# A two-layer graph network with residual norm on one core: x is also read with features on partitions, TensorE turns no rows of it, and each layer has one PSUM pair

## The chip, the cores and the metric

The kernel runs on one core of one Trainium2 chip. The metric is the device time of one execution in microseconds (us). TensorE (PE) multiplies, with its weight loads (PEld) on the side; VectorE (DVE), ScalarE (ACT) and GpSimd (POOL) work elementwise, and SyncE (SP) mostly issues transfers between HBM and SBUF. Each engine has its own queue, which runs strictly in order; engines wait for one another by semaphores.

## What is computed

x has 100000 rows of 256 features; there are 25000 edges, sorted by dst. All is float32.

```python
def _sage_conv(x, src, dst, W_l, b_l, W_r):
    msgs = x[src]
    agg = jax.ops.segment_sum(msgs, dst, num_segments=N_NODES)
    deg = jax.ops.segment_sum(jnp.ones((src.shape[0],), x.dtype), dst, num_segments=N_NODES)
    mean = agg / jnp.maximum(deg, 1.0)[:, None]
    return mean @ W_l + b_l + x @ W_r
...
h = jax.nn.relu(_sage_conv(x, src, dst, W1_l, b1, W1_r))
h = jax.nn.relu(_sage_conv(h, src, dst, W2_l, b2, W2_r))
return h @ W3 + b3
...
x = _layernorm(x + _L0_gnn_ref(...), axis=-1)
```

## The kernel before

Every product is made in three matmuls of a rounded format: each operand is split into a high part (a cast on ACT) and a low part (the operand less its high part, on VectorE), and high × high, low × high and high × low are added in PSUM.

**Stages.** A short first stage splits the weights and works out, from the edge lists, the indices for the gathers, the ends of runs of equal dst, and the reciprocal degrees. The **main stage** handles all 100000 rows as if no edge ended in them: 196 groups g of 512 rows, four groups (slots u = 0 to 3) in each of 49 iterations i. Alongside, every iteration handles one batch of 512 edges: it gathers the rows x[src] and x[dst] (`xe`), turns them, sums the sources over runs of equal dst with a scan (`run`, `mean`), and stores layer-one results for both ends in `h_tab`. The **edge stage** then goes through the 49 batches again, makes layers two and three for the rows with edges, and scatters them over `out`.

**One group in the main stage.** SP loads 512 rows to `xn`. TensorE turns them (8 transposes of 128x128, helper `turn`, L851) into PSUM; ACT casts them to `xt_hi` (L480), VectorE subtracts to `xt_lo` (L645). Layer one is 12 matmuls of 512 columns (helper `columns`, L861). ACT adds the bias and applies relu in two halves to `h_full` in SBUF (L487), casts to `h_hi` (L489), VectorE subtracts to `h_lo` (L649). Layer two is the same again. Layer three is 24 matmuls of 256 columns by rows (helper `by_rows`, L872). VectorE adds `xb` = x + b3, which GpSimd made (L391), to `y` (L671), then takes moments (L683, L694); ACT takes the square root (L493) and normalises to `o` (L500), and SP stores it (L228).

**Order.** The order of each queue is written by hand in the functions named `body`. TensorE's is, for slot u: turn the rows of g+2, layer one of g+1, the edge work of this slot, layer three of g-1, layer two of g. The four PSUM pairs `pair0` to `pair3` rotate: x turned, layer one and layer two of one group lie in the same pair one after another, and edge work and layer three use the other two pairs. The edge work is: turn sources (u=0), turn destinations (u=1), a by-row layer for the sources (u=2, 24 matmuls), one for the destinations with their means (u=3, 48 matmuls). VectorE follows with `low_x` (g+2), `factors` (g-2), `low_h` of layer one (g+1), edge work, residual and moments of g-1, and `low_h` of layer two (g).

Of the kernel before, what the change touches and what calls it, by code (L numbers as in the profile page):

```python
# [5 lines left out]
P = 128  # L6
S = 4
G = S * P
# [5 lines left out]
def build(nc, x, src, dst, W1_l, b1, W1_r, W2_l, b2, W2_r, W3, b3, out):  # L14

# [12 lines left out]
    E = src.shape[0]  # L28
# [3 lines left out]
    NE = -(-E // G)  # L32
    EP = NE * G
    NT = EP // P
    Q = EP // 256
    QF, QR = E // 256, E % 256
    assert NG == NI * U and NE == NI and NT == 2 * Q and N < FAR and QF == Q - 1 and D == 256
    HALF = NE
    MIDDLE = HALF // 2
# [3 lines left out]
    with ExitStack() as ctx:  # L43
# [9 lines left out]

# [12 lines left out]
        xb = sb("xb", [P, 2, S, D])  # L66
        xt_hi = sb("xt_hi", [P, 2, K, G], f32r)
        xt_lo = sb("xt_lo", [P, 2, K, G], f32r)
        h_full = sb("h_full", [P, 2, K, G])
        h_hi = sb("h_hi", [P, 3, K, G], f32r)  # L70
        h_lo = sb("h_lo", [P, 3, K, G], f32r)
# [27 lines left out]
        idx = sb("idx", [P, 3, NT], i32)  # L99
# [4 lines left out]
        e_stage = sb("e_stage", [P, 2, S], i32)  # L104
        t_stage = sb("t_stage", [P, 3, S], i32)

        pair = [pb(f"pair{n}") for n in range(4)]

        pre = h_full[:, :, :, :].rearrange("p a k g -> p (a k g)")
        e_int = pre[0:Q, 0:1024].bitcast(i32).rearrange("p (a j) -> p a j", a=4)  # L110
        fill = pre[:, 1024:1824].bitcast(i32)
        e_f = y[:, :, :, :].rearrange("p a s d -> p (a s) d")[:, 0:4]
        p_src, p_dst, p_prev, p_next = (e_f[0:Q, n] for n in range(4))
        e_w = y[:, :, :, :].rearrange("p a s d -> p (a s) d")
        same, seg_last, count, whole = (e_w[0:Q, n] for n in range(4, 8))
        e_idx = o[:, :, :, :].rearrange("p a s d -> p (a s) d")[:, 0:3]
        tr = o[:, :, :, :].rearrange("p a s d -> p (a s d)")[:, 768:1152].rearrange("p (n c) -> p n c", n=3)
        ones = o[:, :, :, :].rearrange("p a s d -> p (a s d)")[:, 1152:1408]
        rdeg = o[:, :, :, :].rearrange("p a s d -> p (a s d)")[:, 1408:1664]
        rows3 = o[:, :, :, :].rearrange("p a s d -> p (a s d)")[:, 1664:2048].rearrange("p (n c) -> p n c", n=3)  # L120


        w_in, b_in, made, cleared, e_in = (sem(n) for n in ("w_in", "b_in", "made", "cleared", "e_in"))
# [3 lines left out]
        x_in = [sem(f"x_in{u}") for u in range(U)]  # L127
        y_out = [sem(f"y_out{b}") for b in range(2)]
        xt_ps, xhi_ok, xlo_ok = sem("xt_ps"), sem("xhi_ok"), sem("xlo_ok")
# [14 lines left out]
        stage_ok, tab_out, slot_in, slots_ok = (sem(n) for n in ("stage_ok", "tab_out", "slot_in", "slots_ok"))  # L144
# [14 lines left out]
        def after(eng, s, value):  # L159

            if not (isinstance(value, int) and value <= 0):
                eng.wait_ge(s, value)

        def rows(t, g):

            first = min(g * G, N - G) if isinstance(g, int) else g * G
            return t[bass.ds(first, G), :].rearrange("(p s) d -> p s d", s=S)

        def slots_of(t, j, start=0):
# [12 lines left out]

# [9 lines left out]

# [3 lines left out]

# [5 lines left out]
        def _(sp):  # L202
            sp.dma_start(xn[:, 0], rows(x, 0)).then_inc(x_in[0], 16)
            for n, w in enumerate((W1_r, W2_r, W3, W1_l, W2_l)):
                if n == 3:
                    sp.wait_ge(cleared, 5)
                sp.dma_start(w_raw[:, n], w.rearrange("(k p) n -> p k n", p=P)).then_inc(w_in, 16)
            sp.wait_ge(e_in, 16 * 9)
            for n, b in enumerate((b1, b2)):
                for k in range(K):  # L210
                    sp.dma_start(bias[:, n, k:k + 1], b[k * P:(k + 1) * P].rearrange("(p a) -> p a", a=1)).then_inc(b_in, 16)
            for row, b in ((b1_row, b1), (b3_row, b3)):
                sp.dma_start(row[:, :], b.rearrange("(a n) -> a n", a=1).to_broadcast([P, D])).then_inc(b_in, 16)
            for u in range(1, U):
                sp.dma_start(xn[:, u], rows(x, u)).then_inc(x_in[u], 16)

            sp.wait_ge(cleared, 6)
# [7 lines left out]

            def store(g, b):
# [3 lines left out]
            def edge_store(i, u):  # L230

                if u == 0:
                    sp.wait_ge(xdb_ok, i + 1)
                    sp.dma_start(slots_of(xdb_tab, i), xdb[:, :, :]).then_inc(xdb_out, 16)
                if u == 2:
                    sp.wait_ge(src_ok, i + 1)
                    sp.dma_start(slots_of(h_tab, i, EP), src_h[:, :, :]).then_inc(src_out, 16)
                if u == 3:
                    sp.wait_ge(dst_ok, i + 1)
                    sp.dma_start(slots_of(h_tab, i), dst_h[:, :, :]).then_inc(dst_out, 16)  # L240

            def body(i, first, last):
                for u in range(U):
                    g = i * U + u
                    if not last:
                        sp.wait_ge(xt_ps, (g + 1) * K)
                        sp.wait_ge(xb_ok, g + 1)
# [811 lines left out]
```

## Time and profile before

| | |
|---|---|
| median of 3 runs | 2999.09 us (2992.19 to 2999.65) |
| span of the profiled execution, first to last instruction | 2989.1 us |
| mean granted TensorE clock | 0.992 |
| busy, share of the span | PE 96%, PEld 86%, DVE 82%, ACT 67%, POOL 72% |
| main stage | about 35 to 2412 us |
| edge stage | about 2412 us to the end |

The span is measured inside one profiled execution, the median over separate runs of the whole; the difference of 10.0 us is what lies around the instructions. Busy shares are means over stages: what an engine's work is worth has to be read from the stage in which it stands.

### The profile page before, as it was taken

What the parts mean: (1) busy time and instruction counts of PE and PEld (TensorE: products, weight loads), DVE (VectorE), ACT (ScalarE), POOL (GpSimd) and SP (SyncE); (2) the same over time, 40 slices, a digit from 0 to 9 for tenths busy, and PEclk for the clock granted to TensorE, in tenths of its full rate; (3) what the DMA queues carried; (4) which work ended last, traced back from release to release, by engine and by line L of the source; (5) the groups of instructions that cost most, each with busy time, mean ns of one, the idle gap of its engine ahead of it and who ended that gap; (6) DMA issues with size and microseconds to landing.
All of it is one profiled execution on the core that took longest, in us unless ns stands there. A gap on an engine that the chain in (4) does not pass through costs nothing. (4 is left out here: it accounts for less than half of the span.)

```text
span 2989.1 us, 55620 instructions
## 1 busy us (share of the span) xinstructions
PE 2869.4 (96%) x18457; PEld 2581.4 (86%) x18457; DVE 2445.0 (82%) x4001; ACT 1997.4 (67%) x2992; POOL 2151.1 (72%) x1732
## 2 busy tenths in 40 slices
PE   5999999999999999999999999999999989999996
PEld 4888989898888889898988888898989879888885
DVE  5787887879787878878787878788787879899896
ACT  3676766767676767667676767676676746555554
POOL 5777777777776767667777767677777747777776
PEclk9999999999999999999999999999999999999998
DMA  4444444444444445444444444444444366666663
GB/s 131 151 152 145 162 150 149 154 142 161 152 155 148 153 143 165 149 148 154 143 159 154 155 147 153 145 164 149 148 154 145 130 205 232 235 223 226 238 221 141
DMA packets 253121, 488.25 MB, mean 163 GB/s; under 512 B 37615, under 2 KB 165206, under 8 KB 253090
## 3 DMA queue, kind: packets, MB, share of 16 engines
q1 hardware_dynamic: 202498, 387.58, 38.6%
q0 software_dynamic: 50176, 99.91, 10.3%
q10 hardware_dynamic: 416, 0.40, 0.0%
q8 instruction: 14, 0.23, 0.0%
q14 instruction: 17, 0.14, 0.0%
HBM read 284.67 MB, written 206.22 MB: 164 GB/s over the span
## 5 line engine op out<-in xcount | busy, mean ns | idle before, releaser
L487 ACT ACTIVATE h_full<-pair,bias 128x512 f32<-128x512 f32 x784 | 531.6, 685 | 681.2 <-PE pair L861 666.4
L649 DVE TENSOR_TENSOR h_lo<-h_full,h_hi 128x1024 fp32r<-128x1024 f32 x392 | 651.7, 1663 | 188.3 <-ACT h_hi L489 188.2
L391 POOL TENSOR_TENSOR xb<-xn,b_row 128x1024 f32<-128x1024 f32 x196 | 471.5, 2405 | 297.7 <-DVE y L671 295.9
L345 POOL DMA_INDIRECT xe<-in_x_dram,e_stage x392 | 500.9, 1278 | 176.9 <-issue 97.7
L872 PE MATMUL pair<-w_hi,h_hi 128*128 128x256 f32 x1960 | 565.4, 288 | 26.6 <-DVE h_lo L649 24.5
L872 PE MATMUL pair<-w_lo,h_hi 128*128 128x256 f32 x1960 | 555.3, 283 | 0.0
L872 PE MATMUL pair<-w_hi,h_lo 128*128 128x256 f32 x1960 | 555.2, 283 | 0.0
L489 ACT CAST h_hi<-h_full 128x1024 fp32r<-128x1024 f32 x392 | 412.0, 1051 | 12.5
L872 PEld LDWEIGHTS pair<-w_hi,h_hi 128*128 128x128 f32 x1960 | 375.6, 192 | 51.7 <-DVE h_lo L649 47.7
L500 ACT ACTIVATE o<-y,nb,rs 128x256 f32<-128x256 f32 x784 | 407.2, 592 | 5.6 <-DVE nb L702 5.3
L861 PE MATMUL pair<-xt_hi,w_hi 128*128 128x512 f32 x980 | 401.6, 410 | 7.9 <-DVE xt_lo L645 4.3
L861 PE MATMUL pair<-xt_lo,w_hi 128*128 128x512 f32 x980 | 385.4, 393 | 0.0
L861 PE MATMUL pair<-xt_hi,w_lo 128*128 128x512 f32 x980 | 383.9, 392 | 0.0
L872 PEld LDWEIGHTS pair<-w_lo,h_hi 128*128 128x128 f32 x1960 | 376.0, 192 | 1.9
L872 PEld LDWEIGHTS pair<-w_hi,h_lo 128*128 128x128 f32 x1960 | 376.0, 192 | 0.0
L671 DVE TENSOR_TENSOR y<-pair,xb 128x1024 f32<-128x1024 f32 x245 | 298.1, 1217 | 86.6 <-PE pair L872 82.2
L683 DVE BATCH_NORM_STATS2 stats<-y 128x6 f32<-128x256 f32 x980 | 344.0, 413 | 6.8
L851 PE MATMUL pair<-ident,xn 128*128 128x128 f32 x2352 | 306.2, 278 | 43.5 <-DMA xn<-h_tab,h_row 32.8
L851 PEld LDWEIGHTS pair<-ident,xn 128*128 128x128 f32 x2352 | 274.3, 142 | 76.1 <-issue 32.2
L861 PE MATMUL pair<-h_hi,w_hi 128*128 128x512 f32 x784 | 308.0, 393 | 0.0
L861 PE MATMUL pair<-h_hi,w_lo 128*128 128x512 f32 x784 | 307.8, 393 | 0.0
L861 PE MATMUL pair<-h_lo,w_hi 128*128 128x512 f32 x784 | 306.4, 391 | 0.0
(124 smaller groups left out, 6439.6 us busy)
## 6 DMA issues: line engine op xcount, KB each, us to landing
xn<-in_x_dram SPq DMA_DIRECT2D x196, 512.0 KB, 4.0
out_dram<-o SPq DMA_DIRECT2D x196, 512.0 KB, 2.6
seg<-seg_tab SPq DMA_DIRECT2D x74, 512.0 KB, 5.1
xdb_tab<-xdb SPq DMA_DIRECT2D x49, 512.0 KB, 4.8
h_tab<-src_h SPq DMA_DIRECT2D x49, 512.0 KB
h_tab<-dst_h SPq DMA_DIRECT2D x49, 512.0 KB, 6.3
xn<-h_tab SPq DMA_DIRECT2D x49, 512.0 KB, 5.1
xb<-xdb_tab SPq DMA_DIRECT2D x49, 512.0 KB, 4.1
```

The source lines that it names most:

```text
L345: nc.gpsimd.indirect_dma_start(out=xe[:, kind, s], out_offset=None, in_=x, in_offset=bass.IndirectOffsetOnAxis(ap=e_stage[:, kind, s:s + 1 ...
L391: nc.gpsimd.tensor_tensor(xb[:, b], xn[:, u], b3_row[:, :].unsqueeze(1).to_broadcast([P, S, D]), ALU.add).then_inc(xb_ok, 1)
L487: nc.scalar.activation(h_full[:, n, k], ps[:, k], ACT.Relu, bias=bias[:, n, k:k + 1]).then_inc(hf_ok[n], 1)
L489: nc.scalar.copy(h_hi[:, h], h_full[:, n]).then_inc(hhi_ok[n], 1)
L500: ins = nc.scalar.activation(o[:, b, s], y[:, b, s], ACT.Identity, bias=nb[:, b, s:s + 1], scale=rs[:, b, s:s + 1])
L649: nc.vector.tensor_tensor(h_lo[:, h], h_full[:, n], h_hi[:, h].bitcast(f32), ALU.subtract).then_inc(hlo_ok[n], 1)
L671: nc.vector.tensor_tensor(y[:, b].rearrange("p s d -> p (s d)"), ps[:, :, :].rearrange("p k g -> p (k g)"), xb[:, b].rearrange("p s d -> p ...
L683: ins = nc.vector.bn_stats(stats[:, s], y[:, b, s])
L851: ins = nc.tensor.transpose(ps[:, k, s * P:(s + 1) * P], rows_of[:, s, k * P:(k + 1) * P], ident[:, :])
L861: ins = nc.tensor.matmul(ps[:, m], wx[:, w, k, m * P:(m + 1) * P], a[:, k], start=first, stop=end)
L872: ins = nc.tensor.matmul(ps[:, s // 2, s % 2 * D:(s % 2 + 1) * D], a[:, k, s * P:(s + 1) * P], wx[:, w, k], start=first, stop=end)
```

## The change

The host hands the kernel a second copy of x, `xt`, in groups of 512 rows with features on partitions (for the last group, the last 512 rows), so that one transfer per group brings `xtf` as a turn would have left it in PSUM. TensorE's turns of `xn`, and their PSUM space, are gone from the main stage. `xn` is still loaded, for the residual alone, and GpSimd adds b3 to it in place; `xb` is gone.

The four PSUM pairs have fixed uses: `p_l1`, `p_e` (edge work), `p_l2`, `p_l3`. ACT's relu writes back into the pair it reads; cast and subtraction read it from there; `h_full` is gone. Layer one runs two groups ahead of layer two in place of one; the residual on VectorE comes a slot later. `h_hi` and `h_lo` have four buffers in place of three.

Edge indices, the next and previous dst, weights and biases also come laid out by the host, in one transfer each (weights in five); the conversions to float, the six transposes of indices and the staging copies of indices on GpSimd are gone, and GpSimd's main loop is written out. In the last iteration the destination layer moves one slot forward. In the edge stage only buffers have other names, and SP's store of group 194 comes after the first loads.

```diff
-            def turn_rows(i, u, ps):
-                pe.wait_ge(x_in[u], 16 * (i + 1))
-                for k in range(K):
-                    turn(ps, xn[:, u], k).then_inc(xt_ps, 1)
...
             def body(i, first, last):
                 for u in range(U):
                     g = i * U + u
-                    if not (last and u >= 2):
-                        pe.wait_ge(hf_ok[0], (g + 1) * K)
-                        turn_rows(i + (u + 2) // U, (u + 2) % U, pair[u])
-                    if not (last and u == 3):
-                        pe.wait_ge(xlo_ok, g + 2)
-                        edges_left(i, u)
-                        first_layer((u + 1) % 2, pair[(u + 1) % 4])
-                    after(pe, y_ok, g - 1)
-                    edges(i, u, pair[(u + 2) % 4])
-                    if not (first and u == 0):
-                        third_layer(g - 1, pair[(u + 3) % 4])
                     pe.wait_ge(hlo_ok[0], g + 1)
+                    after(pe, hlo_ok[1], g)
+                    second_layer(u % 2)
                     if not (last and u >= 2):
                         pe.wait_ge(xlo_ok, g + 3)
-                    second_layer(u % 2, pair[u])
+                        pe.wait_ge(hlo_ok[0], g + 2)
+                        first_layer(u % 2, p_l1)
+                    if not (last and u == 3):
+                        edges(i, u)
+                    if not (first and u == 0):
+                        third_layer(g - 1, 2 + (u + 1) % 2)
...
             def high_h(g, n, h, ps):
-
                 for k in range(K):
                     act.wait_ge(l_ps[n], g * K + k + 1)
-                    after(act, hlo_ok[n], g)
-                    nc.scalar.activation(h_full[:, n, k], ps[:, k], ACT.Relu, bias=bias[:, n, k:k + 1]).then_inc(hf_ok[n], 1)
+                    nc.scalar.activation(ps[:, k], ps[:, k], ACT.Relu, bias=bias[:, n, k:k + 1]).then_inc(hf_ok[n], 1)
                 act.wait_ge(hf_ok[n], (g + 1) * K)
-                nc.scalar.copy(h_hi[:, h], h_full[:, n]).then_inc(hhi_ok[n], 1)
+                nc.scalar.copy(h_hi[:, h], ps[:, :, :]).then_inc(hhi_ok[n], 1)
...
+            def low_x(g, b):
+                dve.wait_ge(xhi_ok, g + 1)
+                nc.vector.tensor_tensor(xt_lo[:, b], xtf[:, b], xt_hi[:, b].bitcast(f32), ALU.subtract).then_inc(xlo_ok, 1)
```

The other queues of the main loop after the change, each in slot u of group g. ACT: `high_h` of layer two (g), square root (g-2), `high_x` (g+3), `high_h` of layer one (g+2), edge cast, normalise (g-2). VectorE: residual and moments (g-2), `low_h` of layer two (g), `factors` (g-2), `low_x` (g+3), `low_h` of layer one (g+2), edge work.

TensorE, slot u=1 of the loop, before: x turned, layer one, destinations turned, layer three, layer two (a dotted line stands for the remaining matmuls of a layer).

```order
L851 MATMUL pair<-ident,xn 128x128 [waits x_in3,h1f_ok]
L851 MATMUL pair<-ident,xn 128x128 x7
L949 REGISTER_ALU [waits xs_ok,xlo_ok]
L861 MATMUL pair<-xt_hi,w_hi 128x512 [waits run_ok]
...
L851 MATMUL pair<-ident,xe 128x128 [waits xd_in,y_ok]
L851 MATMUL pair<-ident,xe 128x128 x7
L872 MATMUL pair<-w_hi,h_hi 128x256 [waits h2lo_ok]
...
L971 REGISTER_ALU [waits h1lo_ok]
L861 MATMUL pair<-h_hi,w_hi 128x512 [waits xlo_ok]
...
```

The same slot after the change.

```order
L777 MATMUL p_l<-h_hi,w_hi 128x512 [waits h2lo_ok,h1lo_ok]
...
L777 MATMUL p_l<-xt_hi,w_hi 128x512 [waits h1lo_ok,xlo_ok]
...
L834 REGISTER_ALU [waits xs_ok,xd_in]
L768 MATMUL p_e<-ident,xe 128x128 [waits run_ok]
L768 MATMUL p_e<-ident,xe 128x128 x7
L787 MATMUL p_l<-w_hi,h_hi 128x256 [waits y_ok,h2lo_ok]
...
```

The turn of xn is gone; layer two opens the slot, and layer one now waits for h1lo_ok too, that is until VectorE has read the last use of `p_l1`.

VectorE, the first slot of the loop, before.

```order
L645 TENSOR_TENSOR xt_lo<-pair,xt_hi 128x1024 [waits xhi_ok]
...
L649 TENSOR_TENSOR h_lo<-h_full,h_hi 128x1024 [waits h1hi_ok]
...
L719 TENSOR_TENSOR xe_lo<-pair,xe_hi 128x1024 [waits xshi_ok]
...
L671 TENSOR_TENSOR y<-pair,xb 128x1024 [waits l3_ps]
...
L649 TENSOR_TENSOR h_lo<-h_full,h_hi 128x1024 [waits h2hi_ok]
```

The same after the change.

```order
L603 TENSOR_TENSOR y<-p_l,xn 128x1024 [waits l3_ps]
...
L555 TENSOR_TENSOR h_lo<-p_l,h_hi 128x1024 [waits h2hi_ok]
...
L551 TENSOR_TENSOR xt_lo<-xtf,xt_hi 128x1024 [waits xhi_ok]
...
L555 TENSOR_TENSOR h_lo<-p_l,h_hi 128x1024 [waits h1hi_ok]
...
L638 TENSOR_TENSOR xe_lo<-p_e,xe_hi 128x1024 [waits xshi_ok]
```

The residual moves from behind the edge work to the head of the slot, h_lo of layer two from last to second; both h_lo read PSUM now, and xt_lo reads SBUF alone.

## Rows read from the trace of the kernel before

**Rows 1.** The page: busy time, share of the span, instructions.
```profile
PE 2869.4 (96%) x18457; PEld 2581.4 (86%) x18457; DVE 2445.0 (82%) x4001; ACT 1997.4 (67%) x2992; POOL 2151.1 (72%) x1732
```

**Rows 2.** Stretches: length, busy PE, PEld, DVE, ACT, POOL, clock, DMA, GB/s.
```profile
1007.84:1056.17 48.33, 47.89 (x314) 43.20 (x312) 39.36 (x65) 34.08 (x51) 35.13 (x28) 1.00 0.47 152
88.00:2370.00 2282.00, 2260.80 (x14727) 2039.23 (x14726) 1864.62 (x3024) 1610.69 (x2410) 1649.71 (x1275) 1.00 0.46 152
```

**Rows 3.** Waits, 400 to 2300 us: total us, times, longest.
```profile
PEld pair L872 <- DVE h_lo L649: 35.9, 78, 1.0
```

**Rows 4.** Timeline of PE, one iteration: start, us, engine, line, operation.
```profile
1007.84 1.03 PE L851 MATMUL pair<-ident,xn 128*128 128x128 f32 x8
1008.62 0.48 PE L861 MATMUL pair<-xt_hi,w_hi 128*128 128x512 f32 x1
...
1011.45 1.04 PE L851 MATMUL pair<-ident,xe 128*128 128x128 f32 x8
...
1015.46 0.40 PE L861 MATMUL pair<-h_hi,w_hi 128*128 128x512 f32 x1
...
1018.22 1.03 PE L851 MATMUL pair<-ident,xn 128*128 128x128 f32 x8
...
1032.63 0.28 PE L872 MATMUL pair<-w_hi,xe_hi 128*128 128x256 f32 x1
...
1035.51 0.28 PE L872 MATMUL pair<-w_hi,h_hi 128*128 128x256 f32 x1
```

**Rows 5.** Timeline of DVE, ACT and POOL in the same iteration.
```profile
1008.94 2.40 POOL L398 TENSOR_TENSOR xdb<-xe,b_row 128x1024 f32<-128x1024 f32 x1
...
1009.84 2.59 DVE L649 TENSOR_TENSOR h_lo<-h_full,h_hi 128x1024 fp32r<-128x1024 f32 x1 [1.41 <-ACT h_hi L489]
...
1014.92 1.22 DVE L719 TENSOR_TENSOR xe_lo<-pair,xe_hi 128x1024 fp32r<-128x1024 f32 x1
1016.05 2.44 DVE L723 TENSOR_TENSOR_SCAN run<-seg,run,pair 128x512 f32<-128x512 f32 x2
1018.41 1.20 DVE L671 TENSOR_TENSOR y<-pair,xb 128x1024 f32<-128x1024 f32 x1
1019.64 1.40 DVE L683 BATCH_NORM_STATS2 stats<-y 128x6 f32<-128x256 f32 x4
...
1021.45 1.80 DVE L649 TENSOR_TENSOR h_lo<-h_full,h_hi 128x1024 fp32r<-128x1024 f32 x1
...
1018.41 0.69 ACT L487 ACTIVATE h_full<-pair,bias 128x512 f32<-128x512 f32 x1 [0.67 <-PE pair L861]
1019.13 1.05 ACT L489 CAST h_hi<-h_full 128x1024 fp32r<-128x1024 f32 x1
1020.09 1.01 ACT L480 CAST xt_hi<-pair 128x1024 fp32r<-128x1024 f32 x1
...
1024.91 2.08 ACT L500 ACTIVATE o<-y,nb,rs 128x256 f32<-128x256 f32 x4
```

**Rows 6.** Groups by line, 400 to 2300 us: busy us, mean ns, idle before.
```profile
L649 DVE TENSOR_TENSOR h_lo<-h_full,h_hi 128x1024 fp32r<-128x1024 f32 x314 | 521.4, 1661 | 143.6 <-ACT h_hi L489 143.6
...
L645 DVE TENSOR_TENSOR xt_lo<-pair,xt_hi 128x1024 fp32r<-128x1024 f32 x157 | 190.3, 1212 | 0.0
```

**Rows 7.** DMA issues, 400 to 2300 us: KB each, median us to landing.
```profile
xn<-in_x_dram SPq DMA_DIRECT2D x157, 512.0 KB, 4.0
```

**Rows 8.** Timeline of the first 60 us.
```profile
20.74 0.69 DVE L613 CAST y<-h_full 98x1024 f32<-98x1024 int32 x1 [20.74 <-DMA h_full<-in_dst_dram]
...
44.63 0.42 SPq L251 DMA_DIRECT2D seg<-seg_tab  x1
...
51.29 0.47 PE L861 MATMUL pair<-xt_hi,w_hi 128*128 128x512 f32 x1 [3.67 <-DVE run L723]
...
55.70 1.04 PE L851 MATMUL pair<-ident,xe 128*128 128x128 f32 x8
```

**Rows 9.** Timeline at the border between the two stages.
```profile
2404.82 0.99 POOL L429 DMA_INDIRECT xn<-h_tab,h_row  x1 [9.62 <-DMA h_tab<-dst_h]
```

More of the change, by code:

```diff
@@ L27, in build @@
     N, D = x.shape
-    E = src.shape[0]
     K = D // P
@@ L114, in build @@
[L114 to L120, printed above, removed]
@@ L123, in build @@
-        w_in, b_in, made, cleared, e_in = (sem(n) for n in ("w_in", "b_in", "made", "cleared", "e_in"))
+        p_l1, p_e, p_l2, p_l3 = (pb(n) for n in ("p_l1", "p_e", "p_l2", "p_l3"))
+        h_two = xdb[:, :, :].rearrange("p s d -> p (s d)").rearrange("p (k g) -> p k g", k=K)
+        y_w = y[:, :, :, :].rearrange("p a s d -> p (a s) d")
+        same, count, whole = (y_w[0:Q, n] for n in range(3))
+        rows3 = y[:, :, :, :].rearrange("p a s d -> p (a s d)")[:, 1024:1408].rearrange("p (n c) -> p n c", n=3)
@@ L379, in batch @@
-            def batch(i, half, phase):
-                if phase == 0 or (phase == 1 and half == 0):
-                    note_slots(i * 2 + half)
-                else:
-                    look_up(i * 2 + half - HALF)
-            def body(i, first, last, phase):
+                after(pool, slot_in, 16 * S * m)
+                for s in range(S):
+                    t = m * S + s
+                    nc.gpsimd.indirect_dma_start(
+                        out=slots[:, t:t + 1], out_offset=None, in_=slot_tab,
+                        in_offset=bass.IndirectOffsetOnAxis(ap=e_in[:, 0, t:t + 1], axis=0)).then_inc(slot_in, 16)
@@ L393, in body @@
-                    if last and u == 2:
-                        keep_slots(NE - 1)
+                    if g:
+                        add_b3(g)
                     if u == 0:
@@ L802, in residual_edges @@
                 after(dve, c_o_ok, j - 1)
-                residual(j, b, c_l3_ps, c_y_ok, pair[3])
+                residual(j, b, xn[:, b], c_l3_ps, c_y_ok)
             def averages_edges(j, b):
@@ L856, in columns @@
                 first = True
-                for w, hi, lo in parts:
+                for n, hi, lo in parts:
                     for k in range(K):
                         for wx, a in ((w_hi, hi), (w_lo, hi), (w_hi, lo)):
-                            end = k == K - 1 and a is lo and w == parts[-1][0]
-                            ins = nc.tensor.matmul(ps[:, m], wx[:, w, k, m * P:(m + 1) * P], a[:, k], start=first, stop=end)
+                            end = k == K - 1 and a is lo and n == parts[-1][0]
+                            ins = nc.tensor.matmul(ps[:, m], wx[:, n, k, m * P:(m + 1) * P], a[:, k], start=first, stop=end)
                             first = False
```

600 lines of the change are left out of this document (286 added, 314 removed).

## The prediction

> **What bounds the kernel now.** I read the page first. TensorE has rows on it for 96% of the span, VectorE for 82% [rows 1]. Matmuls overlap, so that share alone proves nothing; the stretches and the timeline do. Over the main stage, 88 to 2370 us, TensorE is busy 2260.8 of 2282.0 us at a granted clock of 1.00, VectorE 1864.6 and the 16 DMA engines 46% [rows 2]. One iteration (four groups of 512 rows and one batch of 512 edges) is 48.33 us [rows 2]. In it matmuls start right behind one another: a 512-column layer of 12 matmuls is 2.76 us, start of its first to start of what follows (1015.46 to 1018.22), and a by-row layer of 24 is 2.88 (1032.63 to 1035.51) [rows 4]. Between 400 and 2300 us the only thing that TensorE's loads waited for is h_lo, 35.9 us in 78 waits [rows 3], so twice in an iteration. The main stage is bound by TensorE's instruction stream, with small waits in it.
>
> Pure work in an iteration: four groups of 2.76 + 2.76 + 2.88, one by-row layer of 2.88 for sources, twice that for destinations (48 matmuls), two turns of gathered rows and four turns of x. A turn is 0.78 us (1007.84 to 1008.62), and the layer behind it takes 2.83 instead of 2.76 [rows 4]: 0.85 with that. Sum: 33.60 + 8.64 + 1.70 + 3.40 = 47.34. The 0.99 left of 48.33 is waits.
>
> **What goes.** Four turns of x in each iteration: 3.40 us, on the path, since TensorE has no other idle time to absorb. With the waits gone too the floor would be 43.94. Here one view and one rule part. The eight transposes of a turn print 1.03 us busy and overlap what follows, and the next layer starts after 0.78; the 1568 of x are worth 196 × 0.85 = 167 us by that. The Trainium skill, "TensorE: Matmul & The Clock Gate", section "Part 4: PE-mode transpose", gives about 275 ns for one transpose within a kernel; 1568 of them would be an estimated 431 us. The starts in the timeline decide, and the sum uses 167.
>
> **What moves.** In the new order each slot u of TensorE is second layer of g, first layer of g+2, edge work, third layer of g-1. With one PSUM pair per layer each of these waits for ACT and VectorE to empty the pair that it last filled. So the waits must be walked through. Costs, from start to start, are of the timeline [rows 5]: scans 2.36, residual 1.24, statistics with their aggregates 1.81; a subtraction of 1024 elements 1.13 (1014.92 to 1016.05). On ACT: a relu 0.69, any cast 0.96, normalising 2.08. From the end of a layer on TensorE to the start of the subtraction I take 2.0 us: relu 0.19 after 1018.22, cast 0.72 later, and 1.09 from cast to subtraction. TensorE's slots are 8.40 + 0.90, 0.90, 2.88 and 5.76, thus begin at 0, 9.3, 18.6, 29.9 and end at 44.0.
>
> Slot 0 on VectorE: residual(g-2) 0.2, free at 3.3; h_lo of layer two 4.8 to 5.9; x_lo 6.2 to 7.3; h_lo of layer one 8.2 to 9.3; edge subtraction and scans to 12.8. ACT ends its normalising at 11.0. Slot 1: residual(g-1) starts 3.5 us late at 12.8, its moments end at 15.8; ACT must wait for them before its square root (16.0), and behind that wait are queued x_hi and both relus of g+3. So h_lo of layer one ends at 20.6 only. TensorE wants that at 18.6 + 2.76 = 21.4: 0.8 us to spare, the tightest place. The others: second layer in slot 2 has 1.6, third layer in slot 1 1.7, the turn in slot 1 2.0, edges in slot 2 2.5, the mean's low part in slot 3 2.5. VectorE falls behind in the two short slots (10.2 and 9.0 us of work against 9.3) and catches up in slots 2 and 3. The walk gives no wait. I take 0.4 us per iteration for small errors, so 44.34: 4.0 us less.
>
> A collision could use those 0.8 us. h_lo has both inputs in SBUF and takes 1661 ns on average; xt_lo reads one from PSUM and takes 1212 [rows 6]. At 1009.84 an h_lo took 2.59 us, ending 1.1 us after GpSimd's xdb (1008.94 plus 2.40) [rows 5]. After the change both h_lo read PSUM and x_lo reads SBUF twice: six such subtractions or products per iteration instead of ten. The Trainium skill, "SBUF — State Buffer", section "SBUF: two separate sides", says that a DVE instruction with two SBUF inputs and a GpSimd instruction that reads SBUF block each other for a whole instruction; by that rule, which the two means agree with, x_lo becomes exposed while both h_lo become immune. Cost from both sides: none if they miss, and up to 2.4 us of lateness if x_lo meets a GpSimd add just as it begins; less the reserves, at most 0.6 us of wait in slot 0 or 1. GpSimd no longer waits for y, so its phase is not known beforehand; by the landings (4.0 us for x [rows 7]) it should be issuing gathers when x_lo runs in slots 0 and 1. Its four-element copies go. That makes it lighter than before.
>
> Relu now writes into PSUM. No row shows that. The nearest are relu from PSUM to SBUF 0.69 and casts of 1024 elements, 1.05 from SBUF and 1.01 from PSUM [rows 5]: I take the same 0.69, bounds 0.5 and 1.05 (half of such casts to a whole one). ACT has 34.1 us of work per iteration [rows 2]; 16 relus at +0.36 make 40, still under 44, but in slot 1 they cost 1.5 us on the tight path, so 0.6 of wait.
>
> x transposed is one more 512 KB load per group. One xn load lands in 4.0 us [rows 7]. It is issued after x_lo(g+3) in slot g and wanted by ACT in slot g+2, over 15 us later; on SP it stands ahead of the store that waits for ACT. 12 direct transfers per iteration become 16, so the DMA share of 47% rises to about 0.47 × 16/12 × 48.3/44.3 = 68% at most. Hidden. If it were not, each late microsecond would stand at slot starts.
>
> **Before and behind.** The index work starts on VectorE at 20.74, behind nine transfers; at 51.29 TensorE ends a 3.67 us wait for run, whose seg was issued at 44.63, and at 55.70 it begins the second edge turn [rows 8]. With the laid-out indices I estimate VectorE's index chain 10 to 12 us earlier, seg no longer behind a wait at 44 us, and the second edge turn at 41 to 42, with two layers (5.5 us) more already done: 14 + 5.5, so 20 us gained. Bounds 10 (the seg round trip stays as long) and 30. Between the stages GpSimd waits 9.62 us for the store of dst_h [rows 9], and SP issues the loads of seg only after a store that waits for ACT; that store now stands behind the loads: 3 us, bounds 0 and 8. The edge stage keeps its instructions and orders; only its buffers have other names. 0.
>
> **Sum.** 48.6 iterations remain after the start: 48.6 × 4.0 = 194, plus 20, plus 3, is 217 us. The profiled execution has a span of 2989.1; the runs' median of 2999.1 lies 10.0 above it, and that distance stays. 2999 - 217 = 2782 us.
>
> **Rivals.**
> *A, the forecast*: TensorE's stream remains the bound, waits under 1 us per iteration: 2750 to 2815. The 99% and the walk speak for it. 0.68.
> *B, the short slots fall behind*: ACT waits for moments, VectorE for ACT, TensorE for h_lo, 1 to 3 us per iteration; with 2 us it is 2782 + 48.6 × 1.6 = 2860. For it: only 0.8 us of reserve and a square root that stalls everything behind it. Against: slots 2 and 3 repay, and two h_lo no longer run at 1661. 0.23.
> *C, the front or the stage boundary gives nothing*, or costs some microseconds since seg and the fourth xt load stand in one queue: 2782 + 23 = 2805. 0.06 in its pure form.
> *D, slower than before*: writes of relu to PSUM are slow. 217 us are 4.5 us per iteration. To lose them TensorE would need a period above 48.8, so ACT 14.7 us more over 16 relus: each 1.6 us in place of 0.69. At 1.8 us ACT alone needs 52, and the time is 3000 + 48.6 × 3 = 3145. Nothing in the rows is that slow per element. 0.02.
> *E, the change does not do what it says*: the turns were hidden already. TensorE has no idle time in which they could be. 0.01, time 2980 from the front alone.
>
> **How the numbers follow.** 2782 is A's. Two in ten may lie outside: low 2748 (no waits at all, 213 us, 28 at the front, 8 between), high 2845 (1.7 us of waits per iteration, taking in the nearer part of B). Differences under 0.3% (9 us) can't be told from none. Faster: A, B, C and most of E, 0.97; same 0.01; slower 0.02.
>
> **What would show it.** In the profile after: no transpose of xn or of x in the main stage; an iteration of 43.9 to 44.9 us; TensorE 98 to 99% busy there; no wait for h_lo above 1 us; a wait, if any, ahead of the first layer in slot 2; h_lo at about 1.2 us in every row, x_lo now and then above 2; DMA share 60 to 68%; relu near 0.69; second edge turn before 46 us; an edge stage of the same length. Wrong would be: relu beyond 1.05 us, TensorE waiting for VectorE in slots 1 and 2 for over 1 us, ACT waiting for xt, or an edge stage that changes length.

## The result and the profile after

The changed kernel takes 2852.75 us (median of 4 runs, 2851.62 to 2856.43); the kernel before, measured beside it, 2996.09 (2992.19 to 2999.65). The ratio is 0.9522, 95% interval 0.9508 to 0.9536: 4.8% faster, where 7.2% was forecast, and 7.75 us above the high end of the range. The profiled execution's span is 2850.3 us, 138.8 less than before, at a mean granted clock of 0.99. One execution of `old_order_turnless` below took 9415.95 us, its other four 2914 to 2919, and it is left out of the figures.

The experiments ran on four chips, each time beside the kernel before, whose median there was 2992.5 to 3005.5 us. Where two changed kernels are compared, the surer measure is the difference of their ratios.

The page after: busy time and share, against [rows 1].

```profile
PE 2693.9 (95%) x16883; PEld 2408.5 (84%) x16883; DVE 2461.9 (86%) x3992; ACT 1944.5 (68%) x2993; POOL 1956.3 (69%) x1434
```

TensorE has 1574 matmuls fewer and yet a smaller share of its span. VectorE has nine instructions fewer and 17 us more busy time: something on it got longer. One iteration and a longer stretch, columns as in [rows 2]:

```profile
1045.41:1091.21 45.80, 44.31 (x281) 39.66 (x280) 40.24 (x65) 33.00 (x52) 30.50 (x22) 1.00 0.73 207
100.00:2200.00 2100.00, 2044.92 (x12928) 1830.75 (x12927) 1842.63 (x2960) 1523.94 (x2355) 1424.25 (x972) 1.00 0.68 208
```

The iteration is 45.80 us, not 44.34, and TensorE is idle for 1.49 of it. Over 100 to 2200 us it averages 45.5: about 45.7 up to 1180 us and 45.3 after. The groups of VectorE, 400 to 2200 us, against [rows 6]:

```profile
L555 DVE TENSOR_TENSOR h_lo<-p_l,h_hi 128x1024 fp32r<-128x1024 f32 x317 | 384.4, 1213 | 189.0 <-ACT h_hi L430 189.0
L551 DVE TENSOR_TENSOR xt_lo<-xtf,xt_hi 128x1024 fp32r<-128x1024 f32 x159 | 194.9, 1226 | 0.0
L648 DVE TENSOR_TENSOR mean<-run,seg 128x1024 f32<-128x1024 f32 x40 | 146.3, 3657 | 0.0
L655 DVE TENSOR_TENSOR mean_lo<-mean,mean_hi 128x1024 fp32r<-128x1024 f32 x40 | 106.9, 2672 | 0.0
```

h_lo came down to 1213 ns as forecast, and x_lo is never lengthened (1228 ns at most). But `mean` takes 3657 and `mean_lo` 2672 ns; before the change, from 400 to 2300 us, they took 1215:

```profile
L736 DVE TENSOR_TENSOR mean_lo<-mean,mean_hi 128x1024 fp32r<-128x1024 f32 x40 | 48.6, 1215 | 0.0
L729 DVE TENSOR_TENSOR mean<-run,seg 128x1024 f32<-128x1024 f32 x39 | 47.4, 1215 | 0.0
```

The timeline after the change shows what they overlap (VectorE and GpSimd; start, us):

```profile
1054.29 3.65 DVE L648 TENSOR_TENSOR mean<-run,seg 128x1024 f32<-128x1024 f32 x1
1066.76 3.03 DVE L655 TENSOR_TENSOR mean_lo<-mean,mean_hi 128x1024 fp32r<-128x1024 f32 x1
...
1054.45 2.40 POOL L341 TENSOR_TENSOR xn<-xn,b_row 128x1024 f32<-128x1024 f32 x1
1066.30 2.41 POOL L366 TENSOR_TENSOR xdb<-xe,b_row 128x1024 f32<-128x1024 f32 x1
```

`mean` ends at 1057.94, 1.09 us after GpSimd's addition; `mean_lo` ends 1.08 after xdb. Each lasts about as long as what is left of the addition it meets plus its own work. Not every overlap costs VectorE time: between 400 and 2100 us, 72 executions of h_lo, which has one SBUF input, overlap an addition and none takes over 1.23 us. And x_lo, with two, comes out of the collision unhurt while the addition takes 3.24 us in place of 2.4:

```profile
1154.18 1.23 DVE L551 TENSOR_TENSOR xt_lo<-xtf,xt_hi 128x1024 fp32r<-128x1024 f32 x1
...
1154.42 3.24 POOL L341 TENSOR_TENSOR xn<-xn,b_row 128x1024 f32<-128x1024 f32 x1
```

The recorded starts alone don't say who gives way: mean, which is held in all its 45 executions from 100 to 2150 us, begins 0.14 to 0.17 us before the addition, and this x_lo 0.24 before. What waits for the long means on TensorE and ACT in the same iteration:

```profile
1065.85 0.47 PE L777 MATMUL p_l<-xt_hi,w_hi 128*128 128x512 f32 x1 [0.51 <-DVE h_lo L555]
1069.84 0.39 PE L787 MATMUL p_e<-w_hi,xe_hi 128*128 128x256 f32 x1 [0.98 <-DVE mean_lo L655]
1061.03 0.30 ACT L434 ACTIVATE sd<-mv,eps 128x4 f32<-128x4 f32 x1 [3.99 <-DVE mv L616]
```

And in the list of waits, 400 to 2200 us, against [rows 3]:

```profile
PEld p_e L787 <- DVE mean_lo L655: 41.2, 39, 1.8
```

The two PE waits are the 1.49 us. The first is the walk's tight place (layer one in slot 2: the square root of slot 1 comes late and holds x_hi and both relus), the second is the mean's low part in slot 3.

The front, against [rows 8]: the second edge turn begins at 44.92, not 55.70, and ACT waits once for a transposed load that SyncE issued at 28.84, behind the tables' stores.

```profile
35.79 1.04 ACT L423 CAST xt_hi<-xtf 128x1024 fp32r<-128x1024 f32 x1 [8.75 <-DMA xtf<-in_xt_dram]
40.42 0.76 PE L777 MATMUL p_l<-xt_hi,w_hi 128*128 128x512 f32 x1 [7.57 <-DVE h_lo L555]
```

GpSimd at the border, against [rows 9]:

```profile
2250.97 0.97 POOL L387 DMA_INDIRECT xe<-h_tab,h_row  x1 [18.86 <-DMA h_tab<-dst_h]
...
2273.66 0.95 POOL L387 DMA_INDIRECT xe<-h_tab,h_row  x1 [12.91 <-DMA out_dram<-o]
```

Its two groups of the edge stage (first scan at 2263.65 to the end):

```profile
L395 POOL DMA_INDIRECT out_dram<-o,idx x196 | 224.8, 1147 | 62.8 <-issue 57.2 <-ACT o L509 4.1 <-PE p_l L768 1.5
L387 POOL DMA_INDIRECT xe<-h_tab,h_row x188 | 211.9, 1127 | 81.8 <-issue 56.1 <-DMA out_dram<-o 12.9 <-PE p_l L768 12.8
```

The same two groups of before (2419.66 to the end):

```profile
L437 POOL DMA_INDIRECT out_dram<-o,idx x196 | 218.3, 1114 | 62.6 <-issue 58.5 <-ACT o L570 3.8 <-DMA out_dram<-o,idx 0.3
L429 POOL DMA_INDIRECT xn<-h_tab,h_row x188 | 206.4, 1098 | 77.9 <-issue 55.8 <-PE pair L851 21.8 <-ACT o L570 0.3
```

The span's 138.8 us split so: the front gives 16.3 (10.8, and 5.5 of layers already done), the iterations 139, the way from the last y of the main stage to the first scan of the edge stage 0.9 (7.85 to 6.93), and the edge stage takes 17.2 back (569.4 to 586.6).

### The profile page after: what moved, and what is told of

The parts are those of the page before. It is cut to its first block, busy times and chain, and to the rows that moved or that the text cites. A ratio compares the mean times of both kernels' runs of the same rounds, so it can differ in the third digit from the quotient of the medians.

```text
span 2850.3 us, 50702 instructions
## 1 busy us (share of the span) xinstructions
PE 2693.9 (95%) x16883; PEld 2408.5 (84%) x16883; DVE 2461.9 (86%) x3992; ACT 1944.5 (68%) x2993; POOL 1956.3 (69%) x1434
## 4 chain that ended last, share of the span: by engine, by line
DVE 31%; PE 23%; ACT 17%; issue 15%; POOL 10%; DMA 2%; DVEq 1%; ACTq 0%; POOLq 0%; SPq 0%
PE p_e L787 10%; ACT p_l L428 7%; PE p_l L777 6%; DVE mean L648 6%; PE p_l L787 5%; ACT h_hi L430 5%; POOL xe L387 5%; POOL out_dram L395 5%; DVE stats L609 5%; DVE mean_lo L655 4%; DVE run L642 4%; DVE y L603 4%; ACT xt_hi L423 3%; DVE h_lo L555 2%; DVE src_h L652 2%
## 5 line engine op out<-in xcount | busy, mean ns | idle before, releaser
L555 DVE TENSOR_TENSOR h_lo<-p_l,h_hi 128x1024 fp32r<-128x1024 f32 x392 | 475.3, 1213 | 231.5 <-ACT h_hi L430 231.5
L428 ACT ACTIVATE p_l<-p_l,bias 128x512 f32<-128x512 f32 x784 | 490.7, 653 | 173.4 <-PE p_l L777 172.4
L341 POOL TENSOR_TENSOR xn<-xn,b_row 128x1024 f32<-128x1024 f32 x196 | 493.5, 2518 | 111.0 <-DMA xn<-in_x_dram 108.0
L787 PE MATMUL p_l<-w_hi,h_hi 128*128 128x256 f32 x1960 | 563.1, 287 | 3.5 <-DVE y L603 3.4
L787 PE MATMUL p_l<-w_lo,h_hi 128*128 128x256 f32 x1960 | 555.1, 283 | 0.0
L787 PE MATMUL p_l<-w_hi,h_lo 128*128 128x256 f32 x1960 | 555.0, 283 | 0.0
L777 PE MATMUL p_l<-xt_hi,w_hi 128*128 128x512 f32 x980 | 387.7, 396 | 42.3 <-DVE h_lo L555 33.3
L430 ACT CAST h_hi<-p_l 128x1024 fp32r<-128x1024 f32 x392 | 398.1, 1015 | 12.4
L777 PE MATMUL p_l<-xt_lo,w_hi 128*128 128x512 f32 x980 | 383.9, 392 | 0.0
L777 PE MATMUL p_l<-xt_hi,w_lo 128*128 128x512 f32 x980 | 383.0, 391 | 0.0
```

Source lines behind the costliest of these rows:

```text
L341: nc.gpsimd.tensor_tensor(xn[:, u], xn[:, u], b3_row[:, :].unsqueeze(1).to_broadcast([P, S, D]), ALU.add).then_inc(xb_ok, 1)
L428: nc.scalar.activation(ps[:, k], ps[:, k], ACT.Relu, bias=bias[:, n, k:k + 1]).then_inc(hf_ok[n], 1)
L430: nc.scalar.copy(h_hi[:, h], ps[:, :, :]).then_inc(hhi_ok[n], 1)
L555: nc.vector.tensor_tensor(h_lo[:, h], ps[:, :, :], h_hi[:, h].bitcast(f32), ALU.subtract).then_inc(hlo_ok[n], 1)
L777: ins = nc.tensor.matmul(ps[:, m], wx[:, n, k, m * P:(m + 1) * P], a[:, k], start=first, stop=end)
L787: ins = nc.tensor.matmul(ps[:, s // 2, s % 2 * D:(s % 2 + 1) * D], a[:, k, s * P:(s + 1) * P], wx[:, n, k], start=first, stop=end)
```

## The experiments

**What do GpSimd's additions cost, and do the turns cost what was said?**

`no_add`: the additions of b3 left out of the main stage (so b3 is missing from those rows), a one-column memset in their place.

```diff
-                nc.gpsimd.tensor_tensor(xn[:, u], xn[:, u], b3_row..., ALU.add).then_inc(xb_ok, 1)
+                nc.gpsimd.memset(probe[:, g:g + 1], 0.0).then_inc(xb_ok, 1)
```

> The changed kernel without GpSimd's 196 adds of b3 to x in the main stage (b3 is left out for rows without edges; a one-column memset keeps the order). Theory 1: no collision is left but that with xdb; the iteration goes to 43.9 to 44.3 us and the time to 2765 to 2785 us. Theory 2: the iteration stays above 45 us, the time within 15 us of 2853.

2758.11 us (ratio 0.9175, 0.9159 to 0.9191). mean 1216 ns, iteration 43.76 us: VectorE's long rows are gone with the additions, and the rest of the new order runs without a wait of TensorE. The transposed loads are all still there, so they are not what costs.

`add_later`: the additions kept, two of them moved behind the slot-table instructions.

```diff
-                    if g:
+                    if u in (1, 2):
                         add_b3(g)
...
+                    if g and u in (0, 3):
+                        add_b3(g)
```

> The changed kernel, with two of GpSimd's four adds of b3 per iteration (slots 0 and 3) put behind its eight slot-table transfers instead of ahead of them; nothing is left out. Theory 1 (the two means on VectorE, which read SBUF twice, stand still while GpSimd adds: 3.66 and 3.13 us in place of 1.2): both fall to near 1.2 us, the iteration goes from 45.8 to about 44.2 us, and the time to about 2780 us (2765 to 2800). Theory 2 (the queue orders themselves, ACT waiting for the moments, are the limit): the iteration stays at 45 us or more and the time at 2835 to 2855.

2947.03 us (0.9804, 0.9788 to 0.982): a miss in time. mean and mean_lo fell to 1216 and 1209 ns as the theory said, but the additions now meet `nb`, an operation of 128x4 elements with two SBUF inputs. DVE, then GpSimd:

```profile
1000.75 5.30 DVE L625 SCALAR_TENSOR_TENSOR nb<-mv,rs 128x4 f32<-128x4 f32 x1
...
1001.25 2.41 POOL L341 TENSOR_TENSOR xn<-xn,b_row 128x1024 f32<-128x1024 f32 x1
1003.62 2.40 POOL L366 TENSOR_TENSOR xdb<-xe,b_row 128x1024 f32<-128x1024 f32 x1
```

0.16 us of work took 5.30, through two additions in a row: VectorE does not get in between them. (nb began 0.50 us before the first of them, beside the issue of a transfer on GpSimd; what held it in that half microsecond is not shown.) Behind nb stand the scale and both subtractions. Iterations take 46.0 to 47.8 us, 47.2 on average, and TensorE idles 2.0 us in each, where the changed kernel idles 1.2. That is about half of the lengthening. The rest is busy time at a lower granted clock, 0.97 to 0.98 in each of four stretches of 100 to 2300 us against 1.00; why it was lower is open. So where an addition lands matters more than that it lands.

`turns_back`: eight transposes ahead of each first layer again, of weights, with the result unused.

```diff
+                        for k in range(K):
+                            turn(p_l1, w_raw_rows, k)
```

> The changed kernel with eight transposes put back ahead of each first layer in the loop (of weights, into the pair that the layer then overwrites; their result is not used). Theory 1 and the price of 0.85 us a turn: TensorE had 1.6 to 1.8 us of waits in an iteration, which the turns partly fill, so the iteration goes from 45.8 to 47.3 to 48.0 us and the time to 2925 to 2960 us. Rival (turns add in full, 3.4 us per iteration): 3015 us. Rival (a turn costs 275 ns per transpose, 2.2 us): over 3150 us.

2951.1 us (0.9814, 0.9798 to 0.983), an iteration of 47.43. The changed kernel's 45.80 and four turns of 0.85 would be 49.2; the floor of 43.76 with them is 47.16. TensorE is busy in all of the 2000 us from 100 to 2100 here, so a turn costs (47.43 - 43.76) / 4 = 0.92 us, near the 0.85 of the starts, and the turns take up the waits. They also moved the additions: mean is back at 1216 ns, while mean_lo now stands through two additions in a row and takes 6041 ns. TensorE does not wait for it. A long collision costs nothing where the reserve is larger.

`old_order_xt`: the kernel before with x read transposed from group 2 on and no turns; its order, pairs and relu as before.

> The kernel before with one part of the change alone: from group 2 on x comes in transposed and TensorE turns nothing; queue orders, the four rotating pairs, xb and the index work are as before. If the turns alone carry the gain, the iteration is 48.33 less 3.4, 44.9 us, and the time 2830 to 2840. If the old order cannot follow (layer one only one group ahead, h_lo with two SBUF inputs beside GpSimd's adds), waits for h_lo grow and the iteration stays above 46 us: 2885 or more.

3149.6 us (1.0475, 1.0456 to 1.0493), a miss of my own making: SyncE waited for x_lo ahead of the load of `seg`, and TensorE waited for the scan behind it (164.2 us in 39 waits, 400 to 2400 us). The granted clock was also 0.95 to 0.96 over the main stage, so not all of the loss is the order's. The same with SyncE's xtf load last in its slot:

> The kernel before with one thing of the change: from the third group on x comes in transposed and the turns are left out; order of layers, PSUM pairs and relu as before. Unlike the first try, SyncE loads the next transposed group last in its slot, behind the load of seg. Theory (a turn costs 0.85 us of TensorE's time, 0.35 us of it taken back by collisions and short slots; the first try was slow because seg came 4 us late): seg is no longer waited for, iteration 45 to 47 us, total 2850 to 2930. Rival (leaving out the turns without moving layer one ahead leaves the waits for h_lo and for x_lo exposed, whatever SyncE does): TensorE waits for xt_lo or h_lo in each slot, 3000 to 3150.

2919.34 us (0.9749, 0.9732 to 0.9766). The trace is that of a second run of the same kernel:

> The same kernel as old_order_turnless, for a trace of an undisturbed execution: about 2919 us; the iteration near 47 us; TensorE's remaining waits are for xt_lo or h_lo and for the long means.

2931.99 us (0.9759); iteration 46.53. TensorE's loads wait 86.0 us in 79 waits for h_lo, still with two SBUF inputs (1739 ns). Taking out the turns alone brings 1.8 us of the 3.4 per iteration; the rest of the change (order, pairs, relu, lighter GpSimd) brings up to 2.8 us more when nothing stalls it. Its relu is not needed for that: relu_sbuf, below, also reaches 43.76.

**Is it the place of the additions, and what is the edge stage bound by?**

`add_gated`: each addition waits for a y, xdb for x_lo of slot 3; the slot-table instructions are dealt out three and five.

```diff
+                after(pool, y_ok, g - 2)
...
+                        if i:
+                            pool.wait_ge(xlo_ok, 4 * i + 3)
```

> The changed kernel with its b3 additions kept, but each one held back on GpSimd until VectorE has written a y row block (so that it runs beside statistics and a PSUM-source h_lo), the xdb addition held back until xt_lo of slot 3 is done, and the slot-table instructions spread so that three stand behind the gather of slot 2 and five in slot 3. Theory (only the overlap of a GpSimd addition with a VectorE operation that has two SBUF inputs costs time; its place, not its existence): mean, mean_lo and the small nb all at their undisturbed lengths (about 1.2, 1.2 and 0.16 us), iteration 43.8 to 44.3 us as without the additions, total 2765 (2755 to 2790). Rival one (VectorE has no stretch long enough, the collision just moves to nb or xt_lo as it did with the additions behind the batches): one of these groups has a mean over 1.4 us, 2830 to 2950. Rival two (the additions slow VectorE whatever it reads): h_lo and y get longer, 2810 to 2860.

2764.51 us (0.9235, 0.9213 to 0.9257), as the theory said: mean 1218, mean_lo 1211 ns, iteration 43.76. Between 400 and 2100 us 102 executions of h_lo overlap an addition and none is lengthened, which answers the second rival. One nb in four still meets an addition (1.66 us), in a slot with reserve.

`edge_psum`: in the edge stage relu writes back into PSUM, so h_lo there has one SBUF input; TensorE's next columns wait for h_lo.

```diff
-                nc.scalar.activation(h_two[:, k], p_l2[:, k], ACT.Relu, ...)
+                nc.scalar.activation(p_l2[:, k], p_l2[:, k], ACT.Relu, ...)
...
-                after(pe, c_hf_ok, j * K)
+                after(pe, c_hlo_ok, j)
```

> The changed kernel with only the edge stage altered: the second layer's relu there writes back into PSUM, so h_lo reads PSUM and h_hi, and TensorE's next columns wait for h_lo. Theory (the edge stage's length is that of GpSimd's 384 indirect issues, and an issue is long where it meets a VectorE operation with two SBUF inputs, three per step, of which this removes one): the issues over 1.2 us fall from 90 to about 60, the stage is 20 to 27 us shorter, total 2830 (2824 to 2838). Rival (the stage is set by TensorE or by the scatters' landing; or long issues come of the memory): 2848 to 2865, with the long issues as many as before or TensorE waiting for h_lo.

2824.06 us (0.9438, 0.9416 to 0.9459), 28.7 less than the changed kernel by the medians and 25 by the ratios, at the low edge of what was expected. GpSimd's groups in the edge stage:

```profile
L395 POOL DMA_INDIRECT out_dram<-o,idx x196 | 209.7, 1070 | 67.5 <-issue 56.7 <-ACT o L509 9.2 <-PE p_l L768 1.2
L387 POOL DMA_INDIRECT xe<-h_tab,h_row x188 | 192.7, 1025 | 80.7 <-issue 54.8 <-DMA out_dram<-o 12.7 <-PE p_l L768 12.5
```

34.3 us less busy (436.7 to 402.4), and the stage is 30.8 shorter (586.6 to 555.8), where 20 to 27 was expected. The issues over 1.2 us fall from 90 to 33, not to about 60. In both kernels every one of them overlaps a VectorE operation with two SBUF inputs, and no issue clear of such an operation is that long; but about as many overlap one and stay short (96 in the changed kernel). Which overlaps cost is open.

`gated_edge_border`: both, and GpSimd's wait for the last output stores put ahead of the first scatter (j == 4), where it is needed.

> Both edits above and a third: GpSimd's wait for the last two output stores stands ahead of the first scatter and no longer ahead of the third fetch (12.9 us there in the changed kernel). If the three add up: 2765 less 23 less 8 to 12 = 2732 (2718 to 2755), below both kernels. If the gating only moves the collision: above 2790.

2737.7 us (0.9148, 0.9133 to 0.9164): they add up. The border's part is small: the edge stage is 551.6 against edge_psum's 555.8, 4.2 us where 8 to 12 was expected.

**What is relu in PSUM worth, and the front?**

`relu_sbuf`: the changed kernel with the main stage's relu in SBUF again.

```diff
-                    nc.scalar.activation(ps[:, k], ps[:, k], ACT.Relu, ...)
+                    nc.scalar.activation(full[:, k], ps[:, k], ACT.Relu, ...)
```

> The changed kernel with one part undone: in the main stage relu writes to SBUF again (two buffers in the place of the raw weights), so the high-part cast and h_lo read SBUF alone, as before the change. Theory (what h_lo gained from the change is freedom from the port it shares with GpSimd): h_lo has a mean of 1.5 to 1.8 us in the main stage instead of 1.21, TensorE waits for it, iteration 46.5 to 48 us, total 2890 to 2960. Rival (h_lo's reserve in the new order is large enough to swallow that, the gain came from the order and the turns alone): h_lo long but total 2850 to 2870.

2778.8 us (0.925, 0.9235 to 0.9265): neither theory. Undoing this part makes the kernel 74 us faster (81 by the ratios). Its groups, and below them the timeline of VectorE and GpSimd around mean:

```profile
L562 DVE TENSOR_TENSOR h_lo<-w_raw,h_hi 128x1024 fp32r<-128x1024 f32 x323 | 501.0, 1551 | 156.8 <-ACT h_hi L435 156.8
L655 DVE TENSOR_TENSOR mean<-run,seg 128x1024 f32<-128x1024 f32 x41 | 50.9, 1242 | 0.0
```

```profile
1015.64 1.22 DVE L655 TENSOR_TENSOR mean<-run,seg 128x1024 f32<-128x1024 f32 x1
...
1013.51 1.91 POOL L311 DMA_INDIRECT xe<-in_x_dram,idx  x1 [0.30 <-issue]
1015.72 1.96 POOL L311 DMA_INDIRECT xe<-in_x_dram,idx  x1 [0.30 <-issue]
1017.69 2.43 POOL L342 TENSOR_TENSOR xn<-xn,b_row 128x1024 f32<-128x1024 f32 x1
```

h_lo is long again, but GpSimd's issues are longer too: 1.9 us for 0.95 beside h_lo or mean, and from 100 to 2100 us 410 of 732 are over 1.2 us, where the changed kernel has 176 of 704. The addition behind them starts after mean has ended.

`pool_slower` tries that alone: the changed kernel with two idle memsets on GpSimd ahead of the additions of slots 3 and 0.

```diff
+                    if i and u in (0, 3):
+                        for n in range(2):
+                            nc.gpsimd.memset(w_raw[:, 2 * n:2 * n + 2], 0.0)
```

> The changed kernel with GpSimd given more to do: two idle memsets of 128x1024 (0.97 us each in the front) ahead of the additions of slots 3 and 0, nothing else. If the place in time of the additions is what costs (theory: relu in PSUM shortened GpSimd's issues and let the additions run early, into mean and mean_lo; relu_sbuf was faster because its longer issues push them later), more work on GpSimd makes the kernel faster: the addition of slot 3 starts 2 us later, behind mean; mean back to 1.2 us, total 2760 to 2810. Rival (relu_sbuf was faster for another reason, such as ScalarE's or PSUM's load): the additions are late for nothing, mean or mean_lo stay long, total 2853 or more.

2772.22 us (0.9253, 0.9238 to 0.9269). More work on GpSimd, 80 us less. VectorE, then GpSimd:

```profile
1011.00 1.22 DVE L655 TENSOR_TENSOR mean<-run,seg 128x1024 f32<-128x1024 f32 x1
...
1011.13 1.87 POOL L366 MEMSET w_raw<- 128x1024 f32 x2
1012.94 2.42 POOL L341 TENSOR_TENSOR xn<-xn,b_row 128x1024 f32<-128x1024 f32 x1
```

The memset, which reads nothing, leaves mean at 1.22 us; the addition starts 0.72 after its end.

`xt_early`: the transposed load of group 3 ahead of the tables' stores.

> The changed kernel with one line of SyncE moved: the transposed load of group 3 stands ahead of the stores of the segment tables, not behind them and behind the load of seg. Theory (the front falls 4 us short of its term because xt_hi waits 8.75 us for this load): the wait goes, the second edge turn starts near 38 us instead of 44.92, total 5 to 8 us less, 2846. Rival (the next thing, seg or the gathers, is as late): second edge turn at 43 or later, total within 2 us of the changed kernel.

2848.54 us (0.9486, 0.947 to 0.9502; the changed kernel's interval begins at 0.9508): 4 us less by the medians, 11 by the ratios, with the expected 5 to 8 between them. In the trace ACT's long wait is gone and the second edge turn begins at 37.80.

`all_four`: gated additions, edge stage in PSUM, border, early load.

> The gated additions, the edge stage's relu in PSUM, the later wait at the border, and the early load of group 3 together: 2738 less 5 to 8, 2731 (2726 to 2736).

2729.89 us (0.9088, 0.9073 to 0.9103).

`all_four_sbuf`: the same with the main stage's relu in SBUF.

> The best version so far (additions gated, edge stage in PSUM, border, early load) with the main stage's relu written to SBUF again. Once the additions have a fixed place, what relu in PSUM brings by itself is left: ScalarE's 653 against 677 ns and h_lo clear of GpSimd's port. Theory (TensorE is at 97% of the iteration and h_lo has reserve): within 10 us of all_four, 2725 to 2745. Rival (h_lo meets additions and issues and TensorE waits): 2760 to 2800.

2844.8 us (0.9499, 0.9483 to 0.9515): the rival, and beyond its range. The gate puts additions where h_lo runs, and that h_lo must not have two SBUF inputs. It is 1732 ns, and x_lo, one in four of which now meets an addition, 1954; how much each of the two costs is not separated:

```profile
L569 DVE TENSOR_TENSOR h_lo<-w_raw,h_hi 128x1024 fp32r<-128x1024 f32 x296 | 512.8, 1732 | 85.1 <-ACT h_hi L442 85.1
L564 DVE TENSOR_TENSOR xt_lo<-xtf,xt_hi 128x1024 fp32r<-128x1024 f32 x148 | 289.2, 1954 | 0.0
```

**Which part of the change moved the additions?** Before the change GpSimd's group of additions had spent its idle time waiting for a y (400 to 2300 us):

```profile
L391 POOL TENSOR_TENSOR xb<-xn,b_row 128x1024 f32<-128x1024 f32 x158 | 380.1, 2405 | 238.9 <-DVE y L671 237.4
```

`xb` had two buffers, so an addition could not start until VectorE had used one. Adding in place removed that wait; the small copies of indices on GpSimd (1.19 us for the longest) went too. `gate_only` is the changed kernel with one line, which gives such a wait back:

```diff
             def add_b3(g):
                 u = g % U
+                after(pool, y_ok, g - 2)
```

> The changed kernel with one line added: each addition of b3 on GpSimd waits for a y that VectorE has written (the y of three groups before), as the additions of the kernel before waited for a y; the order of GpSimd's work is untouched, so xdb still follows the addition of slot 0 and may meet nb or xt_lo of slot 3. Theory (the change took away a wait that had held the additions beside y's statistics, and that alone sent them into mean and mean_lo): mean and mean_lo at 1.2 us, total 2758 to 2785. Rival (the slot-table instructions behind the additions, now later, push the next gather or xdb into VectorE's subtractions that have no reserve): 2790 to 2850.

2773.85 us (0.9258, 0.9239 to 0.9277), 79 us less for one wait. The additions lie beside the statistics (GpSimd, then VectorE):

```profile
1018.77 2.41 POOL L342 TENSOR_TENSOR xn<-xn,b_row 128x1024 f32<-128x1024 f32 x1 [2.30 <-DVE y L604]
...
1016.35 1.21 DVE L649 TENSOR_TENSOR mean<-run,seg 128x1024 f32<-128x1024 f32 x1
1017.48 1.21 DVE L604 TENSOR_TENSOR y<-p_l,xn 128x1024 f32<-128x1024 f32 x1
1018.73 1.41 DVE L610 BATCH_NORM_STATS2 stats<-y 128x6 f32<-128x256 f32 x4
```

That the restored wait suffices is shown. pool_slower shows that other work ahead of the additions does it too, so whether keeping the copies alone would have sufficed is open.

`gate_border_early`: the same line with the edge stage in PSUM, the border and the early load.

> The same one line, with the edge stage's relu in PSUM, the later wait at the border and the early load of group 3, so all_four without its rearranged slot-table instructions and without the held-back xdb. If the one line does all of the gating's work: within 5 us of all_four, 2725 to 2740; if the rearrangement mattered: 2745 or more.

2728.28 us (0.9112, 0.9094 to 0.913), not to be told from all_four, and the simpler of the two. Against the changed kernel it is 0.9112 / 0.9522 = 0.957. Its stretch of 100 to 2100 us:

```profile
100.00:2100.00 2000.00, 2000.00 (x12802) 1819.86 (x12802) 1713.97 (x2926) 1506.61 (x2328) 1352.72 (x960) 1.00 0.66 216
```

TensorE has no idle time left there.

## Why the prediction was right in part and wrong in size

**Turns: right.** 3.40 us per iteration, from the starts. The work without waits was put at 43.94 us; the eight kernels without the long means run at 43.75 to 43.77. A turn put back costs 0.92 (turns_back).

**The wait term: the step that failed.** The walk gave no wait, and I took 0.4 us per iteration, 44.34. Measured: about 45.7 in the first half of the main stage and 45.3 later. The iterations gave 139 us, not 194. Of the 78 us by which the four terms together fell short, these are 55. The distance from span to median was 2.4 us and not 10.0, which gave 7.6 back. That 10.0 is not what lies around the instructions, as the section on the time before has it: it set the span of one execution against the median of others, and in the executions here that have both, the time is 1.7 to 3.6 us above the span. The low end, too, was added up wrongly: 213, 28 and 8 from 2999 leave 2750, not 2748. The collision paragraph counted six two-SBUF operations per iteration (four x_lo, mean, mean_lo), then priced only x_lo. It left out nb, which has two SBUF inputs as well. It took GpSimd's phase as open, but looked only for where x_lo would meet it. For the two means it had a reserve (2.5 us at the mean's low part) and no price: up to 2.4 each, plus what mean delays in slot 1. mean late by 2.44 us eats the 0.8 of layer one in slot 2; mean_lo late by 1.8 comes on top of that lateness and eats its 2.5. With both priced, 1.5 to 2 us of waits would have given 2782 + 48.6 × (1.1 to 1.6), 2835 to 2860 us. Rival B named the right place (square root, h_lo, layer one in slot 2) with the wrong cause: the short slots by themselves do not fall behind, as no_add shows.

Behind it stands a line read and not followed. The text says that GpSimd no longer waits for y, and files it under lighter work. That wait had kept the additions behind y and clear of both means; giving it back is worth 79 us. And relu into PSUM, which I credited with making h_lo immune, also shortened GpSimd's issues and let its additions run early: by itself, in this order, it made the kernel 74 us slower (relu_sbuf; 2.7% of the kernel before by the ratios), and with the additions gated it is worth 115 us (all_four_sbuf less all_four; 4.1% by the ratios).

The rule cited in the prediction, of the Trainium skill, "SBUF — State Buffer", section "SBUF: two separate sides", agrees with these rows in what it says of whole instructions: mean at 3657 ns stands through an addition, and h_lo with one SBUF input, in 72 overlaps, through none. Which of two overlapping instructions gives way the recorded starts do not show. What failed was applying the rule to one operation out of three.

**Relu: right.** 653 ns in PSUM, taken as 690. **Transfers: right in time.** Neither TensorE nor ACT waits for one between 100 and 2200 us; the DMA share is 68% over it, though 73% in the iteration shown, above the "68% at most".

**Front: 16.3 for 20.** The missing part is ACT's 8.75 us wait for one load behind the tables' stores; xt_early removes it and starts the turn 7.1 us earlier. **Border: 0.9 for 3.** **Edge stage: 17.2 lost for 0.** I took "same instructions, other names" for "same time". GpSimd's 384 issues fill the stage: 12.0 us of the 17.2 are longer issues (424.7 to 436.7 us), and 5.1 are its waits (26.2 to 31.3). The largest single wait is the 12.91 for output stores; moving it (gated_edge_border) brought 4.2. An issue takes 0.95 to 1.0 us, or up to 2.09 beside a VectorE operation with two SBUF inputs; edge_psum, which removes one of three such operations, shows this to be the bound. Why the same instructions met 90 long issues (over 1.2 us) here, 72 before, and 76 to 99 in the other kernels with this edge stage, is not settled: the two streams' relative phase is my reading, and only argued. The new buffers need not be to blame: the edge stage of the kernel before, untouched, takes 586.0 us with 99 long issues in old_order_xt and 585.0 with 94 in old_order_turnless's trace. So the 17.2 us may be chance as much as the change. The prediction had named an edge stage that changes length as a sign of being wrong, and TensorE waiting for VectorE over 1 us in slots 1 and 2 as another; the first came, and the longest wait, 1.8 us, stood in slot 3.

## What to carry to other kernels

Before a wait is removed from an engine that is off the critical path, ask what it was holding back: here one incidental wait had kept GpSimd's additions clear of two of VectorE's two-SBUF operations. List all such operations with the reserve of each, price the longest collision for every one of them, and if the phase is not known, fix it with a semaphore instead of forecasting it. A part of a change can be worth minus 74 us or plus 115 depending on where another engine's work lies, so undo parts on top of the fix, too.

## What was not expected of the hardware

- A VectorE operation of 128x4 elements took 5.30 us in place of 0.16 while GpSimd ran two additions back to back; it did not get in between. One of 128x1024 took 6.10 in turns_back in the same way, and cost nothing there.
- GpSimd's issue of an indirect transfer is itself lengthened, from 0.95 to as much as 2.09 us, where VectorE runs an operation with two SBUF inputs; its memset neither delayed such an operation nor was delayed (1.87 us for two).
- Adding 1.87 us of idle work twice per iteration to GpSimd took 80 us off the kernel.
